# Self attention's stored query and key parts, laid out by dimension and then head: two transfers a block instead of four

## The reference, cut to what matters

```python
x = _layernorm(x + _L0_attn_ref(x, ...));  x = _layernorm(x + _L0_xattn_ref(x, ctx_512, ctx_512, ...))
x = _layernorm(x + _L0_ffn_ref(x, ...));   x = _layernorm(x + _L1_attn_ref(x, ...))
x = _layernorm(x + _L1_xattn_ref(x, ctx_512, ctx_512, ...));  return _layernorm(x + _L1_ffn_ref(x, ...))

def _L1_attn_ref(x, wq_w, wq_b, wk_w, wk_b, wv_w, wv_b, wo_w, wo_b):   # b 4, l 512, D 256, NH 16, HD 16
    q = (x @ wq_w + wq_b).reshape(b, l, NH, HD)    # k and v likewise
    q = apply_rope(q, pos, ROPE_BASE); k = apply_rope(k, pos, ROPE_BASE)
    # apply_rope: first, second = split(inputs, 2, axis=-1)
    #             concatenate([first * cos - second * sin, second * cos + first * sin], axis=-1)
    scores = jnp.einsum('bnqh,bnkh->bnqk', q, k) / scale
    attn = jax.nn.softmax(jnp.where(causal, scores, jnp.finfo(scores.dtype).min), axis=-1)
    ctx = jnp.einsum('bnqk,bnkh->bnqh', attn, v).transpose(0, 2, 1, 3).reshape(b, l, D)
    return ctx @ wo_w + wo_b
```

## Time and profile before

| what | us |
|---|---|
| runs of the kernel, median of 3 | 1502.89 (1501.14 to 1504.25) |
| the profiled execution: span, the only time that its page gives | 1502.3 |
| PE, DVE, ACT, POOL busy in it | 1372.8, 1064.3, 774.2, 321.4 |
| first matmul of layer 1's self attention | 649.11 after the span's start |

### The profile page before, as it was taken

One profiled execution on the slowest core, in us unless ns is written; L12 is line 12 of the kernel. 1 busy time (PEld: TensorE's weight loads), 2 busy tenths in 40 slices (PEclk: granted clock), 3 DMA queues, 4 the chain that ended last, 5 costly groups with the idle time before them and its releaser, 6 DMA issues. The chain is left out here.

```text
span 1502.3 us, 24918 instructions
## 1 busy us (share of the span) xinstructions
PE 1372.8 (91%) x9358; PEld 763.0 (51%) x9358; DVE 1064.3 (71%) x2351; ACT 774.2 (52%) x1066; POOL 321.4 (21%) x407
## 2 busy tenths in 40 slices
PE   6898899999999989748998889999999999999996
PEld 3565487857898977413444522333333333333285
DVE  4987466661221238767994788999999999997077
ACT  2344366621111102325774315788888888888754
POOL 3110322242000027633434532000000000000011
PEclk9999899999999999958999868999999999999999
DMA  9548633356888832764430660234322234320001
GB/s 340 189 135 247 167 135 121 126 201 215 284 291 296 280 114 64 215 201 125 130 93 24 185 188 1 67 87 104 74 67 67 74 96 93 69 66 2 1 1 57
DMA packets 153353, 198.69 MB, mean 132 GB/s; under 512 B 16235, under 2 KB 125311, under 8 KB 153106
## 3 DMA queue, kind: packets, MB, share of 16 engines
q1 hardware_dynamic: 141516, 165.34, 36.9%
q0 software_dynamic: 9200, 29.64, 6.4%
q10 hardware_dynamic: 2518, 2.13, 0.4%
HBM read 136.08 MB, written 60.70 MB: 131 GB/s over the span
## 5 line engine op out<-in xcount | busy, mean ns | idle before, releaser
L2134 DVE TENSOR_REDUCE xa_part<-psum 128x1 f32<-128x512 f32 (+1 forms) x768 | 462.7, 662 | 21.2 <-PE psum L1987 19.2
L2086 ACT ACTIVATE xa_P<-psum 128x1024 f32<-128x1024 f32 (+1 forms) x416 | 403.4, 1020 | 103.8 <-PE psum L2011 103.0
L2011 PE MATMUL psum<-sa_Q,xa_K 48*128 48x512 bf16 (+3 forms) x1664 | 267.1, 381 | 4.0 <-DMA sa_Q<-xa_mrow 2.9
L1987 PE MATMUL psum<-xa_K,sa_Q 48*128 48x512 bf16 (+1 forms) x768 | 239.4, 388 | 4.5 <-DVE xa_part L2134 1.5
L2027 PE MATMUL psum<-xa_P,xa_V 128*32 128x512 f32 (+1 forms) x1664 | 222.6, 607 | 0.4 <-ACT xa_P L2086 0.4
L1987 PEld LDWEIGHTS psum<-xa_K,sa_Q 48*128 48x128 bf16 x768 | 59.2, 94 | 232.7 <-DVE xa_part L2134 160.8
L2011 PEld LDWEIGHTS psum<-sa_Q,xa_K 48*128 48x128 bf16 (+3 forms) x1664 | 105.3, 97 | 69.1 <-ACT xa_P L2086 21.2
L2131 DVE CUSTOM_DVE_ANT_0 psum<-psum,cf_sb 128x512 f32<-128x512 f32 (+3 forms) x256 | 119.5, 522 | 27.2 <-PE psum L1987 26.6
L1329 PEld LDWEIGHTS psum<-xtT,wgu 128*128 128x128 f32 x992 | 115.5, 192 | 5.8 <-issue 4.6
L1329 PE MATMUL psum<-xtT,wgu 128*128 128x128 f32 x992 | 115.9, 275 | 1.4 <-issue 0.8
L2086 ACT ACTIVATE sa_P<-psum 128x1024 f32<-128x1024 f32 (+3 forms) x128 | 83.4, 702 | 44.0 <-PE psum L2011 43.9
(11 more groups left out here) (245 smaller groups left out, 2169.3 us busy)
## 6 DMA issues: line engine op xcount, KB each, us to landing
wgu<-in_f_gu SPq DMA_DIRECT2D x31, 1024.0 KB, 6.5
xa_K<-kx SPq DMA_DIRECT2D x192, 100.1 KB, 5.1
wdn<-in_f_dn SPq DMA_DIRECT2D x31, 512.0 KB, 6.9
vx<-xv_v SPq DMA_DIRECT2D x48, 256.0 KB, 3.3
xa_V<-vx POOLq DMA_DIRECT2D x16, 768.0 KB, 6.5
sa_Q<-qs SPq DMA_DIRECT2D x64, 96.0 KB, 2.3
sa_K<-ks SPq DMA_DIRECT2D x64, 96.0 KB, 2.3
sa_Q<-qx SPq DMA_DIRECT2D x64, 96.0 KB, 2.3
```

The lines of the kernel that those rows point to most:

```text
L1987: last = pe.matmul(out[:, 0:width], hb.q(u)[tile:tile + HALF, to, qt * P:(qt + 1) * P], hb.k(u)[tile:tile + HALF, to, cut[e]:cut[e] + widt ...
L2011: last = pe.matmul(out(j), hb.k(u)[tile:tile + depth, to, kt * P:kt * P + r], hb.q(u)[tile:tile + depth, to, q0(kt):L], start=(half == 0), ...
L2086: act.activation(Pr[0:r, (u * KT + kt) % PR, h:h + 2, 0:w_], S_PS(p)[0:r, :, 0:w_], ACT.Exp, scale=SCALE).then_inc(s_exp, 1)
L2134: dve.tensor_reduce(part[:, g % 2, col + qt, e:e + 1], src[:, 0:cut[e + 1] - cut[e]], AX, ALU.max).then_inc(s_1free, 1)
```

## The change

The parts are stored in the order sequence, slot, half m, dimension d, head. A block's 128 partitions, now in the order d, head, then lie together in each slot, so that one DMA can hold a run of several slots: `dst` returns one place with the slots as a dimension instead of four places, and `slots` one entry of four slots instead of four of one. `slot_runs` then finds two runs: (high, high) and (mid, low) for a query, the first from one source read twice, and (low, mid, high) and (high) for a key. For the second of these the key's parts lie in the buffer in the order low, mid, high, which `HOMES` says. The reads name the same rows at their new places: 48 rows that lay side by side are now 16 rows of 1 KB apart, the 16 heads of a sequence coming after one another. The weights' columns and the rotary tables are permuted on the host, or laid out, to suit.

```diff
-SLOTS = {"q": (0, 0, 1, 2), "k": (2, 1, 0, 0)}
+HOMES = {"q": (0, 1, 2), "k": (2, 1, 0)}
+SLOTS = {"q": (0, 0, 1, 2), "k": (0, 1, 2, 2)}
...
+    def part(self, n, which):
+
+        return self.parts[:, n % self.ring, self.homes(n)[which], 0:self.width_of(n)]
...
-            act.activation(self.parts[:, u, 0, 0:self.width_of(n)], self.whole[:, u, :], ACT.Copy).then_inc(self.s_hi, 1)
+            act.activation(self.part(n, 0), self.whole[:, u, :], ACT.Copy).then_inc(self.s_hi, 1)
...
-            rows = (env.qs if name == "q" else env.ks).rearrange("(b h s m d) l -> b m s h d l", b=B, h=H, s=len(SLOTS[name]), m=KD)
-            return [rows[b][m][s] for s in range(len(SLOTS[name]))]
+            rows = (env.qs if name == "q" else env.ks).rearrange("(b s m p) l -> b m p s l", b=B, m=KD, p=P)
+            return [rows[b][m]]
...
-        sp_ = Split(env, c_, "sqk", L, bias, dst, lambda n: [(part,) for part in SLOTS[blocks[n][1]]], 4,
+        sp_ = Split(env, c_, "sqk", L, bias, dst, lambda n: [SLOTS[blocks[n][1]]], 4, homes=lambda n: HOMES[blocks[n][1]],
...
-            rows = a.rearrange("(g h r) l -> g r h l", g=GROUPS, h=G)
-            return lambda g, half: rows[g][HD * FIRST_SLOT[name][half]:HD * FIRST_SLOT[name][half] + HALF]
+            rows = a.rearrange("(b r g h) l -> b g r h l", b=B, g=H // G, h=G)
+
+            def rows_of(g, half, odd):
+                first = HD * FIRST_SLOT[name][half]
+                return rows[g // (H // G)][g % (H // G)][first:first + HALF, odd:G:2, :]
+
+            return rows_of
...
-        put(np.tile(table, (2 * P // HD, 1)))
+        put(np.repeat(table, 2 * P // HD, axis=0))
...
-    halves = np.arange(D).reshape(H, 2, HD // 2).transpose(1, 0, 2).reshape(-1)
+    halves = np.arange(D).reshape(H, 2, HD // 2).transpose(1, 2, 0).reshape(-1)
```

More of the change, by code:

```diff
@@ L276, with __init__ @@
 class Split:
-    def __init__(self, env, c, name, width, bias, dst, slots, ring, rope=None, width_of=None):
+    def __init__(self, env, c, name, width, bias, dst, slots, ring, rope=None, width_of=None, homes=None):
         self.env, self.width, self.bias, self.dst, self.rope, self.ring = env, width, bias, dst, rope, ring
+        self.homes = homes or (lambda n: (0, 1, 2))
         self.width_of = width_of or (lambda n: width)
@@ L311, in act_hi @@
             act.wait_ge(self.s_whole, n + 1)
-            act.activation(self.parts[:, u, 0, 0:self.width_of(n)], self.whole[:, u, :], ACT.Copy).then_inc(self.s_hi, 1)
+            act.activation(self.part(n, 0), self.whole[:, u, :], ACT.Copy).then_inc(self.s_hi, 1)
         else:
             act.wait_ge(self.s_full, n + 1)
-            act.activation(self.parts[:, u, 0, 0:self.width_of(n)], ps, ACT.Identity, bias=self.bias(n)).then_inc(self.s_hi, 1)
+            act.activation(self.part(n, 0), ps, ACT.Identity, bias=self.bias(n)).then_inc(self.s_hi, 1)
     def act_mid(self, act, n):
         act.wait_ge(self.s_rest, n + 1)
-        act.activation(self.parts[:, n % self.ring, 1, 0:self.width_of(n)], self.rest[:, n % self.ring, 0:self.width_of(n)], ACT.Copy).then_inc(self.s_mid, 1)
+        act.activation(self.part(n, 1), self.rest[:, n % self.ring, 0:self.width_of(n)], ACT.Copy).then_inc(self.s_mid, 1)
     def dve_rot(self, dve, n, full, ps_a, ps_b):
@@ L335, in dve_rest @@
         if self.rope:
-            dve.tensor_tensor(self.rest[:, u, 0:self.width_of(n)], self.whole[:, u, :], self.parts[:, u, 0, 0:self.width_of(n)],
+            dve.tensor_tensor(self.rest[:, u, 0:self.width_of(n)], self.whole[:, u, :], self.part(n, 0),
                               ALU.subtract).then_inc(self.s_rest, 1)
         else:
-            dve.scalar_tensor_tensor(self.rest[:, u, 0:self.width_of(n)], ps, self.bias(n), self.parts[:, u, 0, 0:self.width_of(n)],
+            dve.scalar_tensor_tensor(self.rest[:, u, 0:self.width_of(n)], ps, self.bias(n), self.part(n, 0),
                                      ALU.add, ALU.subtract).then_inc(self.s_rest, 1)
@@ L351, in pool_lo @@
         pool.wait_ge(self.s_mid, n + 1)
-        pool.tensor_tensor(self.parts[:, u, 2, 0:self.width_of(n)], self.rest[:, u, 0:self.width_of(n)], self.parts[:, u, 1, 0:self.width_of(n)],
-                           ALU.subtract).then_inc(self.s_lo, 1)
+        pool.tensor_tensor(self.part(n, 2), self.rest[:, u, 0:self.width_of(n)], self.part(n, 1), ALU.subtract).then_inc(self.s_lo, 1)
     def sp_out(self, sp, n):
@@ L1716, in load_q @@
                 at, to = base(odd), place(0, half)
-                sp.dma_start(self.q(u)[at:at + HALF, to:to + G // 2, :], self.qp(g, half)[:, odd:G:2, :]).then_inc(self.s_kq[u], 16)
+                sp.dma_start(self.q(u)[at:at + HALF, to:to + G // 2, :], self.qp(g, half, odd)).then_inc(self.s_kq[u], 16)
     def load_k(self, sp, g, u):
@@ L1724, in load_k @@
                     sp.dma_start(self.k(u)[at:at + HALF, to:to + G // 2, :],
-                                 self.kp(g, half)[:, odd:G:2, :]).then_inc(self.s_kq[u], 16)
+                                 self.kp(g, half, odd)).then_inc(self.s_kq[u], 16)
                 else:
@@ L1728, in load_k @@
                         sp.dma_start(self.k(u)[at + j:at + HALF:PROD, to:to + G // 2, :],
-                                     self.kp(g, part)[:, odd:G:2, :]).then_inc(self.s_kq[u], 16)
+                                     self.kp(g, part, odd)).then_inc(self.s_kq[u], 16)
 class LaterQueries:
@@ L2658, in build @@
         weights("1", ctx)
-        stacks = lambda a: lambda g, half: a[half].rearrange("(g h r) n -> g r h n", g=GROUPS, r=HALF)[g]
-        kx_part = lambda g, j: env.kx.rearrange("(g h d) j n -> j g d h n", g=GROUPS, d=HD)[j][g]
+        stacks = lambda a: lambda g, half, odd: a[half].rearrange("(g h r) n -> g r h n", g=GROUPS, r=HALF)[g][:, odd:G:2, :]
+        kx_part = lambda g, j, odd: env.kx.rearrange("(g h d) j n -> j g d h n", g=GROUPS, d=HD)[j][g][:, odd:G:2, :]
         def slots(a, name):
-            rows = a.rearrange("(g h r) l -> g r h l", g=GROUPS, h=G)
-            return lambda g, half: rows[g][HD * FIRST_SLOT[name][half]:HD * FIRST_SLOT[name][half] + HALF]
+            rows = a.rearrange("(b r g h) l -> b g r h l", b=B, g=H // G, h=G)
[3 more added lines that the diff above has]
+            return rows_of
         sa = HeadBuffers(env, ctx, "sa", L, True, slots(env.qs, "q"), slots(env.ks, "k"), env.vs)
```

## The result

The changed kernel takes 1491.45 us (median of 4 runs, 1489.8 to 1492.09) where the kernel before took 1503.18 on the same chip (1501.14 to 1504.25): a ratio of 0.9927, 95% interval 0.9914 to 0.9939, or 11.7 us less. The forecast was 1491.3. The profiled execution took 1491.71, its span is 1489.7. One execution of a later kernel, the changed one with six buffers, took 3363 us; it counts in that kernel's median of 1491.12 (1490.81 without it), but not in its ratio.

The account below looks back on a forecast made before the run. SP's issuing of DMAs was taken to bound the preparation stage. Gains of 10.1 us at its barrier and 1.5 after it sum to 11.6, so 1502.9 falls to 1491.3 us; range 1487 to 1499.

Parts of the forecast that it names:

- SP's list ended the stage: Preparation of layer 1's queries and keys: SP, only issuing DMAs, finishes last, 5.2 us after the slowest computing engine.
- Issues: Block stores on SP: two issues of 0.45 us instead of four, 1.0 us a block, 18 us less over ten blocks.
- Data: Preparation's stores: data engines at 291 GB/s need 36 us, so the stores end about 638.5.
- The engines' chain: ACT, PE, DVE and POOL before the barrier: earlier landing of block 7 brings POOL's drain to 638.55; barrier gain 10.1 us.
- With 1.6 us of idleness instead of 4.9 I take 3.6.: Last key projection on PE before the barrier: it takes 3.6 us instead of 5.37.
- Up to 624 nothing moves: Preparation before 624: earlier buffer waits are hidden by the normalisation, so the engines' times stay.
- the alternative beside the sum: Last key projection before the barrier: if PE's clock stays low, the barrier gain is 8.3 us instead of 10.1.
- Signs: Expected around the barrier: ACT's part waits at most 0.6 us, POOL's drain within 1 us of SP's, PE's first matmul near 639.
- After the barrier: Start of the attention: values and the second group's maxima are issued earlier, gaining 1.5 us, from 0 to 3.7.
- Rival 1: Preparation's stores: queued data hold SP's issues, SP ends at 642.7, gain before the barrier 6 us, time 1497; chance 0.21.
- Rival 2: Block stores on SP: an issue costs what its rows cost, so nothing is won, time 1502.9; chance 0.07.
- Rival 3: Attention's reads at 16 KB steps are slower; at four times the time per row, 28 us lost, time 1531; chance 0.06.

Follow-up runs that it names:

- the fillers: Changed kernel plus matmuls whose results nobody reads, on PE ahead of the last key projection: 1496.03 us with ten, 1491.31 with five.
- the late load: Changed kernel with six part buffers instead of four, and group 2's load moved from the preparation to behind the barrier: 1488.99 us.

## Why the prediction was right

**SP's list ended the stage.** Right, and shown by the kernel before with six buffers.

**Issues, 18 us less for SP.** The price of 0.45 is right where SP isn't held: 0.45 is the median with one slot per issue, 0.466 for the query's two. But ten blocks took 13.0 us (0.89, three times 1.76, 2.07 and 2.76 for two each, 1.06 and 0.96), not 10, most of it because three of them stand behind the values. SP was relieved of 14.7 us. And the reason was only half seen: I credited the count, while most of it is the form of the issue, 0.45 instead of 0.60 at the same size. By the page of the Trainium skill that the prediction weighed (DMA: Bandwidth & Descriptors, "Issuing engines are not separate DMA queues") issuing would usually be too small to matter; the 11.7 us speak against it here.

**Data.** SP's end was put at 637.5 to 639; it came at 640.0, 638.9 in the stage's own time. The data engines moved 266 GB/s between 604 and 638, not over 280, because SP waited for blocks at 607; from 628 on it was 286.

**The engines' chain.** Block 7's landing (624.7), ACT's high part and the start of the last key projection (626.4) came at 624.5 and 626.15, less the offset. (The 0.6 us to land in that sum has no row of its own.) From the rotation to the end of POOL's low part it took 7.1 us as said (633.30 to 640.41), and PE's first matmul stood 0.3 behind POOL's drain. The step that failed is the one between: "With 1.6 us of idleness instead of 4.9 I take 3.6." PE idled 4.70 us and the projection took 6.00. The cause is the sentence "Up to 624 nothing moves": the query projection ended at 622.56, 621.45 in the stage's own time, where before it ended at 624.81. The wait before 624 wasn't hidden. ACT's high part of block 7 had waited 1.55 us for the ring at 610.32, PE 1.93 us behind it, and the key projection of the sequence before took 5.37 at a granted clock of 0.69; with the change the waits there are gone, and it takes 3.67 at 1.00:

```profile
612.55 5.37 PE L1586 MATMUL psum<-xT_sb,s_wk_sb 128*128 128x512 f32 x8 [1.93 <-ACT sv_v L512]
...
612.00 3.67 PE L1591 MATMUL psum<-xT_sb,s_wk_sb 128*128 128x512 f32 x8 [0.26 <-ACT sv_v L517]
```

The first row is of before, the second of after. PE thus ran 3.4 us ahead, 1.7 of it by the clock, and spent the lead waiting for the same copy of V. So the alternative beside the sum came true, 8.3 us ("if PE's clock stays low"), against 8.1 measured. That the slow projection goes with the idle stretch is shown by the fillers, which changed nothing else ahead of it (3.60 and 3.70), and by the kernels in which PE idled 1.72 and 2.50 us (3.67 in both). How much idleness is too much isn't settled: the length of the pause alone doesn't tell, since the row of before above took 5.37 after 1.93 us of it. Signs missed too: ACT's longest waits for a part are 2.86 and 3.36 us, not 0.6; POOL's drain ends 1.8 us after SP's, not within 1; PE's first matmul stands at 641.0 in the stage's own time, not near 639.

**After the barrier.** The term of 1.5 us was too small; 2.6 came. The values are issued 1.6 earlier (1.5 said), but land 1.9 earlier, not 1.1: I had charged their data with waiting for block 14's. Block 15's quicker store, which I left out, gives the maxima row the rest. The two errors, 2.0 us too much before the barrier and 1.1 too little behind it, cancel in part, and what is left, 0.9, is less than two medians of the changed kernel differ by (1491.45 and 1490.24). That the forecast hits to 0.2 us is luck; that it hits to 2 is not.

**The rivals.** Rival 1 (the data engines hold SP) is right in part, behind the values, and too high in its price: a block costs SP 1.3 us on average, not 1.9, and SP ended at 638.9 in the stage's own time, not at 642.7. SP's end becomes the limit once POOL's chain is shortened (639.7 in the stage's own time with six buffers). Rival 2 fell with the issues of 0.466 us at 256 KB. Rival 3 is refuted: a group takes (754.38 - 705.66) / 6 = 8.12 us against 8.24, the share of the data engines is 0.42 against 0.44. Reads at steps of 16 KB cost nothing that shows. The loss at large row pitches that the Trainium skill gives (DMA: Bandwidth & Descriptors, "Latency and other measured facts") doesn't appear at this step; no run here has a larger one.

## What to carry to other kernels

When a queue that only issues transfers ends a stage, look at the form of its issues before their number: rows that lie in one run were a quarter cheaper at the same bytes, and that was most of the gain. When such a queue is shortened, ask which chain ends next and how far behind it is, here 2 us, and let the new arrival times run through every engine's chain: an engine that gets its work earlier may only wait longer, and PE's clock may fall while it does. Microseconds at a barrier need not reach the end. Of 1.0 to 1.6 us won there in three kernels (0.4 to 1.0 against the changed kernel's second profile) no median showed one, though medians of four to six runs that spread over 1.7 to 3.8 us can miss that much; of 3.7 us won by the late load 2.1 showed.

## What the runs showed of the hardware

- One 128 KB store of 1 KB rows takes 0.60 us of SP's queue as 16 x 8 rows that are apart, and 0.45 as 128 rows in one run. A query's two slots, 256 KB, take 0.466, hardly more.
- Right behind a sequence's values (1 MB in four issues), a key block's issues of 384 KB and 128 KB take 0.81 to 0.90 us each; with the block ahead of the values the same issues took 0.36 and 0.52 in the first sequence. In one sequence of three the values then took 0.95 us more.
- The same stage moved 217 GB/s before, 263 after. With the late load, the 12 us from 628 to 640 run at 301 GB/s and a share of 0.97, and with five fillers the 3.6 us from 626.9 at 321 and 0.98, both above the 290 that I had taken for the limit.
